# Dispatch stage of a four-layer kernel: eight context buffers, squares two groups ahead, counts ahead of states, a new order of loads and stores

## The reference, cut to what matters

```python
def _L0_ffn_ref(x, router_w, w1, w2, bias):      # top-2 of 8 experts, rows gathered per expert
    ...
def _hnet_depool(h, h_patch_full, patch_lens):
    h_patch = h_patch_full[..., :D_MODEL]
    bidx = jnp.cumsum(patch_lens, axis=1) - 1
    boundary_mask = boundary_mask.at[jnp.arange(bsz)[:, None], bidx].set(1)
    ...
    _, s = jax.lax.associative_scan(comb, (a_b, u), axis=1)
    plug = jnp.clip(jnp.cumsum(boundary_mask, axis=1) - 1, 0, plen - 1)
    depool_out = depool[jnp.arange(bsz)[:, None], plug]
    return depool_out + h
h = rmsnorm(embeds, g_res)
h = jnp.einsum('bld,ed->ble', h, W_in) + b_in
h_patch = rmsnorm(patch_embeds, g_init)
return _hnet_depool(h, h_patch, patch_lens)
```

## Time and profile before

| | before |
|---|---|
| time, median of 3 runs | 3435.61 us (3434.85 to 3435.68) |
| the profiled execution's own time | 3430.26 us |
| its span | 3428.5 us |
| busy in the span: PE, DVE, ACT, POOL | 2567.7, 2356.4, 1167.4, 920.8 us |
| mean granted clock of PE | 0.884 |
| stage `l0d`, from its first instruction to that of the next stage | 378.31 to 574.26 us |

### The profile page before, as it was taken

How to read it: one execution, slowest core, us unless ns; L and a number is a source line. 1 busy time by engine, 2 the same in 40 slices (tenths; PEclk the granted TensorE clock), 3 DMA queues, 4 the chain that set the end, 5 groups by cost and what they waited for, 6 DMA issues and landing times. The chain is left out here.

```text
span 3428.5 us, 59216 instructions
## 1 busy us (share of the span) xinstructions
PE 2567.7 (75%) x21316; PEld 1670.9 (49%) x21316; DVE 2356.4 (69%) x6032; ACT 1167.4 (34%) x2018; POOL 920.8 (27%) x1305
## 2 busy tenths in 40 slices
PE   2997245899914397997899473996699999769952
PEld 1443234566612266885466341443465555546641
DVE  6998533666547764665677768997666555767768
ACT  0885233433201213112356212772222222226601
POOL 3441422010062260114564203871000000034102
PEclk9998578999957599998999685998799999889975
DMA  3330356222140026665511012100100000011001
GB/s 108 120 118 29 107 191 239 95 75 75 55 136 22 21 91 240 226 226 190 196 51 33 10 49 86 40 28 5 59 9 12 1 1 1 1 48 45 14 12 49
DMA packets 158124, 266.74 MB, mean 78 GB/s; under 512 B 22603, under 2 KB 106105, under 8 KB 151844
## 3 DMA queue, kind: packets, MB, share of 16 engines
q1 hardware_dynamic: 131172, 186.97, 16.3%
q0 software_dynamic: 17904, 76.23, 6.6%
q10 hardware_dynamic: 8784, 0.04, 0.2%
HBM read 175.25 MB, written 88.34 MB: 77 GB/s over the span
## 5 line engine op out<-in xcount | busy, mean ns | idle before, releaser
L1340 ACT ACTIVATE l2e_hf<-l2e_H 128x512 f32<-128x512 f32 x208 | 124.2, 597 | 376.7 <-PE l2e_H L1296 376.7
L1376 DVE CAST l2e_hh<-l2e_hf 128x512 f16<-128x512 f32 x208 | 88.8, 427 | 127.7 <-ACT l2e_hf L1340 112.8
L645 DVE TENSOR_REDUCE l0a_mx<-l0a_S 128x2 f32<-128x512 f32 x256 | 164.4, 682 | 12.2 <-PE l0a_S L487 11.6
L1296 PE MATMUL l2e_H<-l2o_hi,l2e_w 128*128 128x512 f16 x576 | 152.6, 383 | 14.8 <-DVE l2e_w L1352 14.8
L594 ACT ACTIVATE l0a_pf<-l0a_ST 128x512 f32<-128x512 f32 x256 | 145.9, 598 | 41.0 <-PE l0a_ST L501 35.3
L216 POOL TENSOR_TENSOR l3in_n_rstd<-l3in_n_sq,all_mhalf 128x8 f32<-128x8 f32 x4 | 7.1, 1768 | 557.1 <-DVE l3in_n_sq L146 557.1
L1296 PE MATMUL l2e_H<-l2e_hh,l2e_w 128*128 128x512 f16 x640 | 155.1, 379 | 0.0
L641 DVE CUSTOM_DVE_ANT_0 l2s_masked<-l2s_S,l2s_mq 128x128 f32<-128x128 f32 (+1 forms) x512 | 150.7, 349 | 6.3 <-PE l2s_S L487 5.7
L1296 PE MATMUL l1e_H<-l1b_hi,l1e_w 128*128 128x256 f16 (+1 forms) x936 | 145.3, 275 | 7.8 <-DMA l1e_w<-packed,all_second_weight_row 7.8
L1378 DVE TENSOR_TENSOR l2e_hl<-l2e_hf,l2e_hh 128x512 f16<-128x512 f32 x208 | 144.0, 692 | 7.2
L1340 ACT ACTIVATE l0e_hf<-l0e_H 128x512 f32<-128x512 f32 x128 | 76.4, 597 | 207.2 <-PE l0e_H L1296 207.2
(11 more groups left out here) (696 smaller groups left out, 7469.0 us busy)
## 6 DMA issues: line engine op xcount, KB each, us to landing
l0e_wf<-in_L_ffn_w SPq DMA_DIRECT2D x16, 1024.0 KB, 8.0
rows<-l0a_zeros SPq DMA_DIRECT2D x16, 640.0 KB, 6.0
l1u_rb<-rows SPq DMA_DIRECT2D x20, 512.0 KB, 5.4
results<-l1e_y SPq DMA_DIRECT2D x39, 256.0 KB, 3.6
packed<-l0d_wp SPq DMA_DIRECT2D x8, 1088.0 KB
l0a_kv<-in_ctx SPq DMA_DIRECT2D x16, 512.0 KB, 4.2
rows<-l0a_zeros SPq DMA_DIRECT2D x16, 512.0 KB, 5.0
l0d_p_cx<-in_ctx SPq DMA_DIRECT2D x16, 512.0 KB, 4.1
```

Of the source, the lines that this page charges most:

```text
L645: m = nc.vector.tensor_reduce(mx[h % 2][:, :, i], ps[:, :].rearrange("p (u k) -> p u k", u=TB), AX.X, ALU.max)
L1296: mm = pe.matmul(bank[0:fn, :], W[par][0:kn, at + k * wd + f0:at + k * wd + f0 + fn], X, start=(done == 0), stop=(done == k_all - 1))
L1340: nc.scalar.activation(hf[q % 4][0:fn, :], pair_of(q, lay)[0][0:fn, :], lay.func, scale=1.0 / WS).then_inc(acted, 1)
L1376: nc.vector.tensor_copy(high, v).then_inc(hi_done, 1)
```

## The change

The stage keeps all its work. What changes:

- `RING` is 8: eight context buffers, and a fetch waits for `u_done` of batch b-8. The sums of squares and the roots get one column per tile of their own, so squares wait for no root.
- ACT makes squares of batches 0 to 3 at the start, and in turn e those of 2e+4 and 2e+5. DVE's `mean` is shifted with them: `mean(e+2)` stands first in turn e. `mark` runs two batches ahead, not one.
- PE issues `count(t+1)` ahead of `states(t)`.
- SP: the weights of experts 0 and 1 are loaded before context 4 to 7. In turn e it fetches 2e+8 and 2e+9, stores `packed` of e, loads the weights of e+2, then stores `pooled` of batches 2e-3 and 2e-2 (before: 2e-5 and 2e-4, behind the store of e-1).
- DVE makes `lo_parts` of the send first. POOL clears only the last 256 columns of the weight buffers (the part that a load leaves unwritten), and does it first.

```diff
-    RING, GROUP = 4, 2
+    RING, GROUP = 8, 2
...
-        self.ss = [st.sb(f"p_ss{i}", [P, self.GROUP * TB]) for i in range(2)]
-        self.rstd = [st.sb(f"p_rstd{i}", [P, self.GROUP * TB]) for i in range(2)]
+        self.ss, self.rstd = st.sb("p_ss", [P, NT]), st.sb("p_rstd", [P, NT])
...
+        count(0)
         for t in range(B + 1):
+            if t + 1 < B:
+                count(t + 1)
             if t < B:
-                count(t)
                 states(t)
             if t >= 1:
                 gather(t - 1)
...
-            q = b // self.GROUP
-            if b % self.GROUP == 0 and q >= 2:
-                act.wait_ge(self.roots, q - 1)
...
                 depool.vectors(sp)
-                for b in range(depool.RING):
+                for b in range(2 * G):
                     depool.fetch(sp, b)
                 pack.begin_move(sp)
+                pack.load(sp, 0)
+                pack.load(sp, 1)
+                for b in range(2 * G, depool.RING):
+                    depool.fetch(sp, b)
                 for e in range(E1):
-                    pack.load(sp, e)
                     for b in range(G):
                         depool.fetch(sp, e * G + b + depool.RING)
-                    if e:
-                        pack.store(sp, e - 1)
+                    pack.store(sp, e)
+                    if e + 2 < E1:
+                        pack.load(sp, e + 2)
                     for b in range(G):
-                        depool.store(sp, (e - 2) * G - 1 + b)
-                pack.store(sp, E1 - 1)
-                for b in range((E1 - 2) * G - 1, B):
+                        depool.store(sp, (e - 1) * G - 1 + b)
+                for b in range((E1 - 1) * G - 1, B):
                     depool.store(sp, b)
...
                 send.hi_parts(nc, act)
-                for b in range(G):
+                for b in range(2 * G):
                     depool.square(act, b)
                 for e in range(E1):
                     for b in range(G):
-                        depool.square(act, (e + 1) * G + b)
+                        depool.square(act, (e + 2) * G + b)
                     pack.hi_part(act, e)
...
+                send.lo_parts(nc, dve)
                 depool.begin_vector(dve)
-                send.lo_parts(nc, dve)
+                depool.mark(dve, 0)
+                depool.mark(dve, 1)
                 depool.mean(dve, 0)
-                depool.mark(dve, 0)
+                depool.mean(dve, 1)
                 for e in range(E1):
-                    depool.mean(dve, e + 1)
+                    depool.mean(dve, e + 2)
                     for b in range(e * G, (e + 1) * G):
-                        depool.mark(dve, b + 1)
+                        depool.mark(dve, b + 2)
                         depool.plugs(dve, b)
                         depool.scale(dve, b)
                     pack.lo_part(dve, e)
...
+        rest = self.mats[-1][1]
         for v in self.wf:
-            nc.gpsimd.memset(v[:, :], 0.0).then_inc(self.zeroed, 1)
+            nc.gpsimd.memset(v[:, self.cols - rest:self.cols], 0.0).then_inc(self.zeroed, 1)
```

More of the change, by code:

```diff
@@ L1616, in root @@
         pool.wait_ge(self.means, q + 1)
-        self.g.nc.gpsimd.tensor_tensor(out=self.rstd[q % 2][:, :], in0=self.ss[q % 2][:, :],
-                                       in1=self.g.mhalf[:, 0:self.GROUP * TB], op=ALU.pow).then_inc(self.roots, 1)
+        v = slice(q * self.GROUP * TB, (q + 1) * self.GROUP * TB)
+        self.g.nc.gpsimd.tensor_tensor(out=self.rstd[:, v], in0=self.ss[:, v], in1=self.g.mhalf[:, v], op=ALU.pow
+                                       ).then_inc(self.roots, 1)
     def on_tensor(self, pe):
@@ L1668, in square @@
             act.wait_ge(self.cx_in[b % self.RING], (b // self.RING + 1) * 16)
-            q = b // self.GROUP
-            if b % self.GROUP == 0 and q >= 2:
-                act.wait_ge(self.roots, q - 1)
             for k in range(TB):
-                if b or k:
-                    act.wait_ge(self.squares, b * TB + k)
-                i = b % self.GROUP * TB + k
+                i = b * TB + k
+                if i:
+                    act.wait_ge(self.squares, i)
                 self.g.nc.scalar.activation(self.squared[:, :], self.cx[b % self.RING][:, k, :], ACT.Square,
-                                            accum_out=self.ss[q % 2][:, i:i + 1]).then_inc(self.squares, 1)
+                                            accum_out=self.ss[:, i:i + 1]).then_inc(self.squares, 1)
     def keep_state(self, act, b):
@@ L1727, in mean @@
             dve.wait_ge(self.squares, (q + 1) * self.GROUP * TB)
-            self.g.nc.vector.tensor_scalar(self.ss[q % 2][:, :], self.ss[q % 2][:, :], 1.0 / DC, RMS_EPS,
-                                           ALU.mult, ALU.add).then_inc(self.means, 1)
+            v = slice(q * self.GROUP * TB, (q + 1) * self.GROUP * TB)
+            self.g.nc.vector.tensor_scalar(self.ss[:, v], self.ss[:, v], 1.0 / DC, RMS_EPS, ALU.mult, ALU.add
+                                           ).then_inc(self.means, 1)
     def mark(self, dve, b):
@@ L1762, in scale @@
         for k in range(TB):
-            i = b % self.GROUP * TB + k
+            i = b * TB + k
             m = self.g.nc.vector.scalar_tensor_tensor(self.u[b % 2][:, k, :], self.cx[b % self.RING][:, k, 0:D],
-                                                      self.rstd[q % 2][:, i:i + 1], self.gain[:, :],
+                                                      self.rstd[:, i:i + 1], self.gain[:, :],
                                                       ALU.mult, ALU.mult)
@@ L2106, in _ @@
             def _(pool):
+                pack.fill(nc)
                 depool.begin_pool(pool)
-                pack.fill(nc)
                 def between(t):
```

## The result

| | before | after |
|---|---|---|
| time, median | 3435.64 us (4 runs, 3434.85 to 3437.27) | 3393.64 us (4 runs, 3390.65 to 3398.27) |
| ratio | | 0.9881, 95% interval 0.9867 to 0.9895 |
| the profiled execution's own time and span | 3430.26 and 3428.5 us | 3398.27 and 3396.5 us |
| stage `l0d`, first instruction to that of the next stage | 195.95 us | 159.09 us |

The kernel is 42 us faster, 1.2%. The forecast was 3399 us, in a range of 3385 to 3413. In the profiles the stage is 36.9 us shorter (36.2 less were forecast for its end), but the spans differ by 32.0 and the timed medians by 42.0. One of the 7 executions of before that were timed with the second set of kernels took 9390.38 us, at a mean granted clock of 0.321, and no ratio uses it.

What follows compares the result with a forecast made beforehand. It took a loop of waits, not an engine or bandwidth, as the bound. Start 402, turn 0 16.4, turns 1 to 4 75.2 and tail 44.5 end the stage at 538.1, 36.2 us less: 3399.4 us, range 3385 to 3413.

Steps and rivals of the forecast that it cites:

- turn 0: First expert's turn, with no gather in its first half: 3.25, 3.3, 6.3 and 3.56, together 16.4 us.
- turns 1 to 4: The four expert turns after the first, each with a mean, at 18.8 us: 75.2 us in all.
- last mean: DVE's final `mean`, now opening turn 5 instead of 6, at 493.6 us on the profile's clock.
- tail: From the final `mean` to the next stage: batches of 5.7 us (states, gather, take, u), 44.5 us in all.
- rival 1: Stores of `pooled`, queued behind weights and `packed`, still hold `keep`: 10 to 20 us lost, time 3409 to 3419; chance 0.16.
- The loop stays closed: `mean(e+2)` still stands first in DVE's turn and waits for ACT's squares, so 3.25 and 3.56 us stay per turn.
- The turn of 18.8: A turn with a mean costs 3.25 + 6.27 + 1.5 + 4.19 + 3.56 = 18.8 us.
- Counts ahead of states: On PE: bound and plug leave the path, but take still waits for the gather; gain 1.6 us per turn.
- Stores a turn earlier: On SP: `pooled` stores issued a turn earlier hide ACT's 49.3 us of waits for landings, 0 to 6 us to spare.
- The start: `mean(2)` waits for contexts 4 and 5 behind two experts' weights: at 402, not 397.41, 4.6 us lost.
- POOL: Its 64 scatters, slowed 2.3 us by each of 8 `lo_part`s, finish at 524, 14 us inside the end: cost nothing.
- From the stage to the median: The stage's 36.2 us gain in the profile was subtracted whole from the timed median: 3435.61 - 36.2 = 3399.4.

Runs made afterwards that it cites:

- four buffers: After with `p_take` in four buffers, not two, so `plugs(b)` waits for the gather of b-4: stage 145.08 us, time 3379.03 us, ratio 0.9844.

## Why the prediction was right

| term | forecast | measured (first profile of after) |
|---|---|---|
| `mean(2)` | 402 | 402.53 |
| turn 0 | 16.4 | 14.1 |
| turns 1 to 4 | 4 x 18.8 = 75.2 | 19.7, 18.4, 19.4, 18.4: 75.9 |
| last mean | 493.6 | 492.53 |
| tail | 44.5 | 45.3 |
| next stage starts | 538.1 | 537.85 |
| PEclk in the first half of turns 1 to 4 | about 0.67 | 0.65, 0.76, 0.67, 0.78 |
| DMA share over the stage | 0.69 (rival 1) | 0.70 |
| ACT's waits for landings | under 5 | 6.7, in two |
| last scatter | ends at 524 | issued at 515.5, ends at 518.9 |
| median | 3399.4 | 3393.64 |

The mechanism held, term by term. That the end came within 0.3 us of the sum is partly luck: `mean(2)`, turns 1 to 4 and the tail were 0.5, 0.7 and 0.8 us later or longer than forecast, and turn 0 was 2.3 us shorter.

- *The loop stays closed* (first part): right, and shown. Moving the mean behind the turn's scales opened it and gave 35 us. One group ahead instead of two cost 5 us of the stage, where I had expected about 1.
- *The turn of 18.8*: right as a mean (19.0) and in no single turn. I took 6.27 and 1.5 us, 7.8, from the first states to the second; they were 8.7 and 8.4 in turns 1 and 3, and 7.4 in turns 2 and 4, by how long PE ran at the low clock.
- *Counts ahead of states*: right. The gather holds `p_take`; PE's idle time before the second states of a turn fell from 2.92 to 1.35 us in turn 1, the 1.6 of the forecast, and from 2.7 to 1.35 to 1.46 in the others, 1.2 to 1.3. Counts alone gave 11.5 us, and the rest of the wait, taken away with four buffers, 14.0.
- *Stores a turn earlier*: right. The order of SP alone gave 17.1 us, and later stores on after cost nearly the whole gain. Rival 1 didn't come true, though the DMA share rose as it said: no `keep` of turns 1 to 5 waited for a landing. The 4.21 us at 516.43 were not forecast and moved nothing: the batches around them follow each other in 5.7 us.
- *The start*: right in place and size; 3.8 us for 1.08 MB. The bounds were added up wrongly: `mean(2)` from 399 to 407 around 402 gives 31 to 39 us less, not 33 to 41.
- *Turn 0* was mis-sized: 14.1 in place of 16.4. I priced the states and the gather of its second half at the low clock; `states` of batch 1 followed those of batch 0 without a gap, and PE had reached the full clock by then (0.62 us for their first matmuls at 408.96, where the low clock takes 1.22).
- *POOL*: right that it did not count. Four of the 8 `lo_part`s met a scatter, not all as I had costed: beside the other four POOL issued none. Those four took 3.44, 3.08, 2.43 and 3.36 us. The Trainium skill (SBUF — State Buffer, Who interferes with whom) has such a DVE instruction take only the read side of the shared port pair, and infers that descriptor generation needs the write side. These four scatters waited all the same. A scatter also reads its row numbers (`all_first_write`); which of its accesses waited, no run shows.
- *From the stage to the median*: the weak step. I took before's profile for typical ("I move the median by what the profile would move"). Its stage was the shortest of three, by 5 and 11 us, since PE's clock had held in the gaps of its tail and, against the third, in turn 1. A part of the gain that I had at zero is that behind the shorter gap PE began at the full clock every time. With it the median fell by 42.0 us, where the profiled stage fell by 36.9 and I had forecast 36.2.

## What to carry to other kernels

Preparing work further ahead doesn't shorten a loop while the instruction that waits for it stays ahead of the turn's other work on its engine: look at where the wait stands, not at how early its data are needed. When a wait is taken away, read all the conditions of the next instruction; here two waits of one function hung on one gather, and only the smaller part went. Profile the kernel before more than once ahead of making a sum against it: here three profiles had stages of 196, 201 and 207 us.

## What the runs showed of the hardware that was not expected

- The same idle gap of 2.7 us in PE was followed by the full clock in one execution of before and by the low one in another. Within the first profile both occur: the first matmuls behind such a gap took 1.22 us at 524.65, though the counts just ahead of it (0.38 us) had run at the full clock, and 0.70 us at 549.50. In the two profiles of after, gaps of 1.35 to 1.57 us were never followed by the low one, gaps of 6.6 us always.
- A scatter of POOL that ran beside DVE's two-input `lo_part` ended 0.84 to 0.85 us behind it, four times in the first profile of after: 2.43 to 3.44 us, not 0.97, the longer the earlier it met the `lo_part`. All 64 together took 77.6 us against 72.3.
